# The projection ahead of the pair pass of a graph network: one product of 258 columns for each 128 nodes, through four banks in turn

## The reference, cut to what matters

```python
hihj = jnp.concatenate([x[src], x[dst]], axis=-1)
exp_e = jnp.exp(_silu(_bn(hihj @ Wf + bf, f_gamma, f_beta)))      # one score of an edge
we = weight[src] * exp_e
a = we / segment_sum(we, dst)[dst]
z = jnp.einsum('ed,hdk->ehk', hihj, Wg) + bg                      # 128 values of an edge
z = _silu(_bn(z, g_gamma, g_beta))
h = segment_sum(a * z, dst)
out = _bn(h, n_gamma, n_beta) + x
```

## Time and profile before

| | us |
|---|---|
| median of 3 runs | 11310.89 |
| lowest and highest of them | 11306.09, 11317.72 |
| the profiled execution | 11313.72 |
| span of its trace, first to last instruction | 11311.9 |
| mean granted clock of TensorE, whole span | 0.597 |
| in the trace: the stage of the change (scaling of chunk 0 to the last copy out of a bank) | 8403.7 to 8539.8 |
| in the trace: first gather of the pair pass | 8545.2 |

### The profile page before, as it was taken

The page is one execution under the profiler, slowest core; times in us unless marked ns, Lnnn a source line. Parts: engine busy times, 40 slices in busy tenths (PEclk is TensorE's granted clock), DMA queues, the critical chain, the costliest instruction groups (busy, mean ns, idle before and its releaser), DMA issues. The chain is left out here.

```text
span 11311.9 us, 80457 instructions
## 1 busy us (share of the span) xinstructions
PE 4272.0 (38%) x19462; PEld 2951.7 (26%) x19462; DVE 3426.1 (30%) x7384; ACT 3212.1 (28%) x7261; POOL 8218.0 (73%) x8365
## 2 busy tenths in 40 slices
PE   1222222342222223223333433333354433344687
PEld 0111111121111112111111333333354333333576
DVE  4000001110001112000000422222235677777898
ACT  3333333343333334333333300000021111111465
POOL 5777777757777775777777677777766777777676
PEclk5555555565555556555555655566665555555799
DMA  4222222222222223222222222221214555555453
GB/s 104 79 79 79 79 79 79 75 87 79 79 79 79 79 79 101 79 79 79 79 79 79 62 53 53 53 53 53 53 47 136 159 159 165 164 166 168 148 170 134
DMA packets 676194, 1069.57 MB, mean 95 GB/s; under 512 B 150850, under 2 KB 518729, under 8 KB 648857
## 3 DMA queue, kind: packets, MB, share of 16 engines
q0 software_dynamic: 329072, 676.05, 22.9%
q10 hardware_dynamic: 247712, 225.10, 6.1%
q1 hardware_dynamic: 98985, 163.50, 4.4%
HBM read 904.63 MB, written 161.05 MB: 94 GB/s over the span
## 5 line engine op out<-in xcount | busy, mean ns | idle before, releaser
L448 POOL DMA_INDIRECT big<-table_parts,tile_cols x4689 | 4436.4, 946 | 1591.0 <-issue 1427.4
L601 PE MATMUL psum<-big 128*128 x4992 | 1723.0, 505 | 4113.0 <-SPq L457 3659.4
L601 PEld LDWEIGHTS psum<-big 128*128 128x128 bf16 x4992 | 672.0, 141 | 5094.2 <-issue 2874.0
L448 POOL DMA_INDIRECT big<-ptable,tile_cols x1563 | 1500.8, 960 | 498.4 <-issue 476.0
L448 POOL DMA_INDIRECT big<-table,tile_cols x1563 | 1480.1, 947 | 478.5 <-issue 476.0
L556 ACT ACTIVATE big<-big,ones 128x2048 bf16<-128x2048 bf16 x312 | 624.4, 2001 | 3689.3 <-PE psum L601 2458.7
L549 ACT ACTIVATE big<-iota_col,dl_tab 128x128 bf16<-128x128 f32 x4992 | 1490.6, 387 | 33.4 <-PEq L725 12.9
L1612 PE MATMUL psum<-acc,big 128*128 x3328 | 784.5, 418 | 1211.2 <-DVE big L1588 1199.1
L578 DVE TENSOR_REDUCE acc<-psum 128x128 f32<-128x384 f32 (+1 forms) x196 | 109.7, 560 | 3635.1 <-PE psum L604 1820.3
L673 PE MATMUL psum<-big 128*128 x3328 | 752.8, 419 | 1194.1 <-SPq L457 740.7
L1612 PEld LDWEIGHTS psum<-acc,big 128*128 128x128 f32 x3328 | 700.8, 315 | 1294.7 <-issue 1294.3
(11 more groups left out here) (299 smaller groups left out, 4284.9 us busy)
## 6 DMA issues: line engine op xcount, KB each, us to landing
big<-dl_rows ACTq DMA_DIRECT2D x104, 1024.0 KB
zrows<-big ACTq DMA_DIRECT2D x104, 1024.0 KB, 5.5
big<-zrows SPq DMA_DIRECT2D x104, 1024.0 KB, 4.9
big<-table_parts,tile_cols POOLq DMA_INDIRECT x4689
table_parts<-big SPq DMA_DIRECT2D x42, 672.0 KB, 3.5
big<-table,tile_cols POOLq DMA_INDIRECT x1563
big<-ptable,tile_cols POOLq DMA_INDIRECT x1563
ptable<-big SPq DMA_DIRECT2D x14, 455.0 KB, 4.1
```

Of the source, the lines that this page charges most:

```text
L448: pool.indirect_dma_start(out=slots[:, t % (groups * GT), 0:width], out_offset=None, in_=tab, in_offset=bass.IndirectOffsetOnAxis(ap=idx_t ...
L601: last = nc.tensor.matmul(held, m, rows_t, start=False, stop=False, skip_group_check=True)
```

## The change

For each window there is now one product of 258 columns, source half with its score and destination half with its score, in a bank of its own. Window k takes bank 4 + k % 4. `s_proj` goes up with each product. The engines that take the results out go window by window: ScalarE takes windows 0, 2, 4 and 6, VectorE windows 1, 3 and 5, each with two copies of 129 columns, and each raises its semaphore (`s_kept1`, `s_kept2`) with each window (VectorE's last of a chunk by two, so that both count to 4 in a chunk). The products of windows 4, 5 and 6 wait until window 0, 1 or 2 of the same chunk has been taken out of their bank. The separate copies of scores are gone, and ScalarE's copy of the node weights stands ahead of its windows and no longer behind.

```diff
             def _(dve):
                 def keep_projections(c, h, c2):
-                    gate(dve, (s_proj, c + 1), (s_stored_of[h], 16 * c2))
-                    for b in range(2, 4):
-                        k0, k1 = ZSPLIT[b]
-                        nc.vector.tensor_copy(pstage[h][:, k0:k1, 0:F], projections(b, 0))
-                        nc.vector.tensor_scalar(windows(acc, c * CW + k0, k1 - k0), projections(b, 1), 0.0, None, ALU.add)
-                    nc.vector.tensor_copy(pstage[h][:, :, F], scores[:, :, 0])
-                    nc.vector.tensor_scalar(acc[:, bass.ds(c * CW, CW), F], scores[:, :, 1], 0.0, None, ALU.add).then_inc(s_kept2, 1)
+                    for k in BY_DVE:
+                        gate(dve, (s_proj, CW * c + k + 1), *([(s_stored_of[h], 16 * c2)] if k == BY_DVE[0] else []))
+                        nc.vector.tensor_copy(pstage[h][:, k, 0:SCW], projection(k, 0))
+                        nc.vector.tensor_scalar(acc[:, bass.ds(c * CW + k, 1), 0:SCW].rearrange("p w f -> p (w f)"), projection(k, 1),
+                                                0.0, None, ALU.add).then_inc(s_kept2, 2 if k == BY_DVE[-1] else 1)
...
                 def project(c, h, _):
-                    after(pe, (s_hkept, c + 1), (s_kept1, c), (s_kept2, c))
-                    for b, (k0, k1) in enumerate(ZSPLIT):
-                        for k in range(k0, k1):
-                            of_t = h_t[h][:, k * F:(k + 1) * F]
-                            nc.tensor.matmul(z_banks[b][:, (k - k0) * 2 * F:(k - k0 + 1) * 2 * F], of_t, w_z[:, :, 0:F], start=True, stop=True)
-                            last = nc.tensor.matmul(scores[:, k, :], of_t, w_z[:, :, F], start=True, stop=True)
-                    last.then_inc(s_proj, 1)
+                    kept = KEPT * c
+                    after(pe, (s_hkept, c + 1), (s_kept1, kept), (s_kept2, kept))
+                    for k in range(CW):
+                        if k >= PROJ_BANKS:
+                            freed = BY_ACT if k % 2 == 0 else BY_DVE
+                            gate(pe, (s_kept1 if k % 2 == 0 else s_kept2, kept + freed.index(k - PROJ_BANKS) + 1))
+                        nc.tensor.matmul(bank[4 + k % PROJ_BANKS][:, 0:2 * SCW], h_t[h][:, k * F:(k + 1) * F],
+                                         w_z[:].rearrange("p a f -> p (a f)"), start=True, stop=True).then_inc(s_proj, 1)
...
                 def keep_projections(c, h, c2):
-                    gate(act, (s_proj, c + 1), (s_stored_of[h], 16 * c2))
-                    for b in range(2):
-                        k0, k1 = ZSPLIT[b]
-                        nc.scalar.copy(pstage[h][:, k0:k1, 0:F], projections(b, 0))
-                        nc.scalar.copy(windows(acc, c * CW + k0, k1 - k0), projections(b, 1))
-                    nc.scalar.copy(pstage[h][:, :, SCW], dyn(node_w, c * CW, CW)).then_inc(s_kept1, 1)
+                    after(act, (s_stored_of[h], 16 * c2))
+                    nc.scalar.copy(pstage[h][:, :, SCW], dyn(node_w, c * CW, CW))
+                    for k in BY_ACT:
+                        gate(act, (s_proj, CW * c + k + 1))
+                        nc.scalar.copy(pstage[h][:, k, 0:SCW], projection(k, 0))
+                        nc.scalar.copy(acc[:, bass.ds(c * CW + k, 1), 0:SCW].rearrange("p w f -> p (w f)"), projection(k, 1)).then_inc(s_kept1, 1)
```

More of the change, by code:

```diff
@@ L1404, in gnn_kernel, with projection @@
         pstage = [ring_flat[:, h * CW * ACW:(h + 1) * CW * ACW].rearrange("p (w f) -> p w f", f=ACW) for h in range(2)]
[L1406 to L1412, removed]
-            k0, k1 = ZSPLIT[b]
-            return z_banks[b][:, 0:2 * F * (k1 - k0)].rearrange("p (w a f) -> p w a f", a=2, f=F)[:, :, part, :]
+        BY_ACT, BY_DVE = [range(k, CW, 2) for k in range(2)]
+        PROJ_BANKS = 4
+        KEPT = len(BY_ACT)
+        assert len(BY_DVE) == KEPT - 1
+        def projection(k, part):
+            return bank[4 + k % PROJ_BANKS][:, part * SCW:(part + 1) * SCW]
         ln = LayerNorm(2, is_node, lambda c, h, k: h_out[h][:, k * F:(k + 1) * F])
@@ L1491, in keep_h @@
                 def keep_h(c, h, _):
-                    gate(act, (s_htr, c + 1), (s_proj, c - 1))
+                    gate(act, (s_htr, c + 1), (s_proj, CW * (c - 1)))
                     keep_transposed(h_t[h], s_hkept)
                 def keep_projections(c, h, c2):
-                    gate(act, (s_proj, c + 1), (s_stored_of[h], 16 * c2))
-                    for b in range(2):
-                        k0, k1 = ZSPLIT[b]
-                        nc.scalar.copy(pstage[h][:, k0:k1, 0:F], projections(b, 0))
-                        nc.scalar.copy(windows(acc, c * CW + k0, k1 - k0), projections(b, 1))
-                    nc.scalar.copy(pstage[h][:, :, SCW], dyn(node_w, c * CW, CW)).then_inc(s_kept1, 1)
+                    after(act, (s_stored_of[h], 16 * c2))
[4 more added lines that the diff above has]
+                        nc.scalar.copy(acc[:, bass.ds(c * CW + k, 1), 0:SCW].rearrange("p w f -> p (w f)"), projection(k, 1)).then_inc(s_kept1, 1)
                 skewed(act, (2, lambda c, h, _: ln.root(act, c, h)), (0, keep), (3, keep_h), (2, relu), (4, keep_projections))
@@ L1507, in store @@
                 def store(c, h, _):
-                    gate(sp, (s_kept1, c + 1), (s_kept2, c + 1))
+                    kept = KEPT * (c + 1)
+                    gate(sp, (s_kept1, kept), (s_kept2, kept))
                     sp.dma_start(node_rows(ptable, c), pstage[h]).then_inc(s_stored_of[h], 16)
```

## The result

The changed kernel takes 11332.29 us (median of 16 runs, 11329.09 to 11335.18), the kernel before 11312.56 (16 runs, 11306.09 to 11317.72): a ratio of 1.0017, with a 95% interval of 1.0009 to 1.0025. It is 19.7 us slower. Forecast were 11324, a range of 11304 to 11350, and a change of less than 0.2% with a chance of 0.75.

A forecast was written before the change was run, and what follows sets the result against it. A TensorE-ScalarE loop, 8.08 us a step, was taken to bound the stage. Terms +9.9, +1.6, -3.3, -5.6, -0.9 made +1.7; clock +11.4 made +13.1: 11326.8 profiled, 11324 as median, range 11304 to 11350.

The forecast's parts named there:

- The loop of the kernel before: Stage's full step: set by a loop over TensorE and ScalarE, summed to 8.06 us; keep_h and relu cost nothing.
- The product: TensorE's project: 258 columns take 0.435 us a window, so seven windows take 3.05 us in place of 4.50.
- The copies: ScalarE's 129-column copies out of a bank: 0.16 us to the next, 0.27 to the end, 0.43 a window's pair.
- The wait ahead of window 4 and the new step: TensorE idles 2.8 us until ScalarE, behind relu, empties window 0; step 9.07 us, +9.9 over ten steps.
- The drain: Stage's last steps: 14 and 15 +1.6 us, step 16 -3.3, step 17 -5.6, last copy -0.9.
- The clock: TensorE's granted clock falls after the idle time in steps with a relu: +11.4 us, between bounds 0 and +46.
- case C: TensorE's clock is low in most of the stage: from +23 to +48 us, chance 0.17.
- The sum: Whole kernel: +1.7 us at a high clock plus 11.4 for the clock, +13.1 against the profiled execution.
- A: TensorE waits for relu and loses its clock for part of each step: +13.1 us, range +7 to +22, chance 0.52.
- B: The same wait of TensorE for relu, but the clock stays high: +1.7 us, chance 0.23.
- D: TensorE is not made to wait, step some 6.5 us: -28 us in all, 11283, chance 0.08.
- The rival that the handshake costs: Stage: more, shorter copies and more semaphores cost the time, about +20 us in the follow-up forecasts; no chance given.

The follow-up runs named there:

- short relu: Six of seven relu activations of each chunk left out: in the changed kernel 0.998 of the kernel before, in the kernel before 1.0005.
- gap-filled: Changed kernel with three extra unread 512-column products on TensorE ahead of window 4, in chunks with a keep_h: 1.0006 and 1.0003 of the kernel before.
- two-product: Changed kernel with two products a window again, 256 and 2 columns, into the same bank: 1.0028 of the kernel before.
- first-three-windows: Changed kernel with ScalarE copying windows 0 to 2 ahead of relu, VectorE windows 3 to 6: 0.999 and 0.9988 of the kernel before.
- relu last: ScalarE's relu put behind its keep_projections copies: in the changed kernel 1.0047 of the kernel before, in the kernel before 1.0042.

## Why the prediction was right, point by point

*The loop of the kernel before.* Right. The short relu left it at 8.09 us a step, so `relu` was off it.

*The product.* 0.435 us forecast for 258 columns; four of them take 1.75 us in the gap-filled run (8460.11 to 8461.86) and the two-product step is 0.62 longer. Right.

*The copies.* Pair to pair 0.32, end after 0.42 to 0.43 (8456.35 to 8456.77). Right.

*The wait ahead of window 4 and the new step.* Forecast 2.8 us and 9.07, measured 2.60 to 2.67 and 9.05. Right, and the short relu shows the cause: with `relu` cut in the same way, one kernel gains and the other does not.

*The drain.* Step 16, -3.3 forecast and 8.10 - 4.81 = -3.3 measured. Step 17 and the last copies, -6.5 forecast; 8529.49 to 8539.76 before and 8552.56 to 8556.39 after are -6.4. Right for this pair of traces, but 4.1 us of it are the low clock of step 17 in the one execution that was profiled. The second trace of before does not have it. The sum was made against an execution whose stage was 5.2 us longer than that of another one, and it was then carried to the median by the difference of the total times, 2.8 us, which is no measure of this stage. This is the term that was mis-sized: the drain saves about 5.7 us against the undisturbed one and not 9.8. Three pairs agree: after, gap-filled and first-three-windows stand in their medians 4 to 7 us higher against before than in their stages against the first trace.

*The clock.* A quarter of the full price, +11.4, forecast. Measured: (10.26 - 9.05) x 9 = 10.9 us over steps 5 to 13, and 13 us for the whole stage by filling the gap. The granted clock was 0.88 against a forecast of 0.75 to 0.95. The size was a choice between far ends, 0 and +46, and that it came out near was luck: nothing in the trace of before had fixed it. The rule of the Trainium skill ("TensorE: Matmul & The Clock Gate", "Loop structure matters more than you think") is that the loop nest decides whether matmuls stay at full clock, and its bad example has a long wait for a DMA ahead of every matmul. It holds here in direction, for a wait of 2.67 us for a copy, but not as all or nothing: two of nine steps kept 2.4 GHz over such a gap, and in the others the clock was back within a step, which is why case C, low throughout, did not come. The price of the 84 more semaphore increments stays open, since no run changes them alone.

*The sum.* Forecast for the profiled pair +13.1, measured +14.6 in the stage. The median moved by 19.7; the 5 us between are the trace of before. The time itself, 11332.3, is 8.3 above the 11324 forecast: 1.7 because the median of 16 runs of before lies that much above the median of three, about 4 for the drain, about 2 for the clock. These errors all have the same sign; the range was wide enough to hold them.

*The cases.* A came about, near the upper end of its own range (+7 to +22). B is what the gap-filled kernel does: +1.7 forecast for a clock that stays high, +1.6 and +1.3 measured in the stage against the same trace. D was priced at 6.5 us a step; the short relu gives 7.75 and the first three windows 7.34, because VectorE is next in line, which that price left out. Its direction is confirmed: without the wait the change is a gain.

*The rival that the handshake costs.* Falls: the first-three-windows kernel has the same copies and semaphores and is faster than both.

Left open: what decides in which step the clock falls, and why the two-product kernel lost more of it with a shorter gap.

## What to carry to other kernels

A finer handshake pays only where the engine that frees the buffer is free to do so. Before splitting a wait, read from the timeline when that engine reaches the first piece, and put the pieces that are wanted first, and ahead of its long phase, on the engine that comes first. Here that turned 20 us slower into 11 to 14 us faster with the same copies. Follow such a reordering through every engine, since the loop that closes need not run over the two that were looked at. And a gap that is opened on TensorE has two prices, its length and the clock; work that fills it, even useless work, tells them apart. Where a sum leans on a short stretch of one trace, take a second trace of it.

## What the runs showed of the hardware

The clock of TensorE fell after an idle time of 1.62 us in one execution of the kernel before and kept 2.4 GHz after the same 1.62 us in another; over gaps of 2.6 to 2.7 us in the kernel after, two of nine full steps have windows 4 to 6 in 1.54 us and the others in 2.4 to 2.9.

VectorE's operations on 128x7 elements of the norm factors (lines 377 and 379) take 0.17 us when GpSimd stands still. One that starts while GpSimd works on `xs` or `acc` ends 0.01 to 0.03 us behind GpSimd's operation, in this stage of the traces of before, after and relu last without exception, and so takes up to 1.82 us; in the rows of the run with relu last they are 1.75 and 1.60. VectorE's reciprocal of the same size (line 375) takes 0.20 at 8492.17, beside a GpSimd operation that runs from 8492.15 to 8494.23, so it is not held up. Off the loop this costs nothing; with relu last, with or without the new dealing out of the windows, it stood on it.
